# Squares to ScalarE, one power for 16 heads, routing in ten units, and the last batch's list and scatters moved into the experts

## The chip, the cores and the metric

The kernel runs on one core of one Trainium2 chip. The metric is the device time of one execution in microseconds (us); lower is better. A core has five engines with a queue of instructions each, worked off in order: TensorE (PE; its weight loads are listed as PEld), VectorE (DVE), ScalarE (ACT), GpSimd (POOL) and SyncE (SP), which issues transfers. They wait for each other by semaphores. GpSimd issues the indirect transfers (scatters) itself.

## What is computed

Four layers on X of 4 batches x 512 tokens x 256 columns: linear attention, a mixture of experts, softmax attention, and the same mixture again, each added to X. Cut to what matters here:

```python
# linear attention, 16 heads of 16 columns, chunks of 128 tokens
o = o * sigmoid(gate)
og = o.reshape(b, n, num_heads, hd)
og = og * rsqrt(mean(og * og, axis=-1, keepdims=True) + EPS)
x = x + (og.reshape(b, n, d) * w) @ Wo
# mixture of experts on layernorm(x): 32 experts, top 8 of a softmax, kept up to a mass of 0.8
logits = h @ gate_weight.T
combine = ...                      # weight of every token at every expert
for w_gu, w_d, ce in experts:
    g, u = split(h @ w_gu.T)
    acc = acc + (silu(g) * u) @ w_d.T * ce[:, None]
x = x + acc
```

## The kernel before

There are four stages, each with a block of its own and a barrier behind it: `lightning` (linear attention), `experts` "f", `attention`, `experts` "g".

`lightning` works through 4 batches (B) of 4 chunks (TT) of 128 tokens. A chunk has 4 units (QUADS), one for four heads, so there are 64 units, and 11 more in the drain (DRAIN), in which only `finish` and `route` run. Every engine has its own loop over the units; in a unit it does, in this order, its part of the scores, of `finish` and of the next half batch's projection, and then `route`. A chunk c is finished over the units of the following chunks: in unit 0 (q == 0) behind it ScalarE copies its outputs `o_t` (line 517); in unit 1 TensorE transposes them (434) and VectorE multiplies by the gate, `og` (709); in unit 2 GpSimd squares, `sq` (600); in unit 3 VectorE sums by head, `ss` and `ms` (723, 728). A chunk later GpSimd raises `ms` to -0.5, `rrms`, heads 0 to 7 in unit 0 and heads 8 to 15 in unit 1 (594); VectorE scales, `og` by `rrms` and `og_norm` by the weights, in unit 2 (715, 720); TensorE transposes `og_norm` in unit 3 (442) and ScalarE and VectorE split it into `og_t.hi` and `og_t.lo` (522, 697); TensorE multiplies by Wo, y (133), and VectorE adds it to X (702).

Score masks (`q_mask`) are made by GpSimd up to unit 39 and by ScalarE from unit 40 on (BY_ACT, lines 527 to 534 and 576 to 585).

The routing of a batch (`Routing`) is a list of steps 0 to 16. Step 0 and 2 are the layernorm (VectorE), step 1 its power `rstd` (GpSimd, 981), 4 and 5 transposes (TensorE, ScalarE), 6 the logits, 7 the softmax (ScalarE's exponential at 1032), 8 the choice, 9 and 10 the weights, 11 the counts (TensorE), 12 the rows' places `index` (VectorE, 1143 to 1152), 13 the tiles' counts, 14 to 16 the list of tiles that the experts read (`list_tiles`). In `lightning` batch f starts at unit 16 (f + 1) + 10, one step a unit (`steps_at`); 28 scatters (ALL) put its rows into `expert_rows` in DRAM (989), two a unit from 13 units after its start (PLACED). Batch 2's list and its first 8 scatters lie in the drain. The experts scatter the 20 left and route batch 3 beside their first pairs (`together`, `scatters_at` in `program`).

`experts` computes 144 tiles of 128 rows in 72 pairs. SyncE loads rows (1399), up to 8 pairs ahead. Three lists (PHASES) cover pairs 0 to 11, 12 to 25 and 26 to 71; the first needs the scatters of batches 0 and 1, the second those of batch 2, the third those of batch 3 and 32 stores of pad rows that SyncE issues four a pair from pair 17 on (1408). Results stay in a ring of 19 entries (RESULTS) until GpSimd scatters them, two scatters a pair (1304). GpSimd's queue in this stage is: power of batch 3, the scatters left of batch 2, the 28 of batch 3, then the results of pairs 0 to 60. VectorE (line 1540) waits before pair u until the results of pair u - 19 have landed:

```python
def wait_free(self, eng, u):
    if u >= RESULTS:
        eng.wait_ge(self.scattered[self.at(u)], 32 * (u // RESULTS))
```

## Time and profile before

| | us |
|---|---|
| median of 3 runs | 1091.12 |
| lowest and highest of them | 1089.68, 1091.18 |
| profiled execution, its own time | 1090.43 |
| span of that execution in the trace | 1088.70 |

Over the span TensorE is busy 877.9 us (81%), GpSimd 642.1 (59%), VectorE 583.0 (54%), ScalarE 544.2 (50%). These shares are means over stages with different limits. In the page's 40 slices of 27.2 us the first stage fills slices 0 to 10; in slices 9 and 10 TensorE is busy 2 and 5 tenths and its granted clock is 0.9 and 0.5 of full speed, while GpSimd is busy 7 to 8 tenths. In a timeline a row gives the start in us, the duration, the engine, the line in the kernel, the operation with output and input, and in brackets the engine's idle time before it and what ended that time. Rows of waits give the instruction that waited, what it waited for, the total in us, how often, and the longest.

### The profile page before, as it was taken

How to read it: one execution, taken by the hardware profiler on the slowest of the kernel's cores; microseconds unless marked ns; L12 is line 12 of the kernel's file. 1: busy time of each engine (PE TensorE's matmuls, PEld its weight loads, DVE VectorE, ACT ScalarE, POOL GpSimd, SP SyncE). 2: the span in 40 equal slices, each digit the busy share in tenths (PEclk: the TensorE clock that was granted, in tenths of full speed). 3: DMA queues.
4: the chain of work that ended last, by engine and by line, in shares of the span. 5: the costliest groups of instructions: out<-in, count | busy, mean ns of one | idle time of the engine just before them, and what ended most of it. 6: DMA issues, size and time to landing. Idle time of an engine off the chain costs nothing. (4 is left out here: it accounts for less than half of the span.)

```text
span 1088.7 us, 20645 instructions
## 1 busy us (share of the span) xinstructions
PE 877.9 (81%) x5504; PEld 665.9 (61%) x5504; DVE 583.0 (54%) x2104; ACT 544.2 (50%) x1084; POOL 642.1 (59%) x636
## 2 busy tenths in 40 slices
PE   5999998971489899999368998988758998999940
PEld 4666665641388699998233443544327887999830
DVE  4566785775373222226776488765535522222665
ACT  6333446640145455555268776766423554556520
POOL 2466648787577777775730010373754777777770
PEclk9999999995599999999679998988887999999975
DMA  9600002162578887773540110135326888778776
GB/s 335 252 1 2 1 20 91 67 240 78 168 233 301 281 267 220 222 259 123 174 136 35 34 35 35 49 121 215 116 103 200 261 303 280 227 218 255 270 243 204
DMA packets 93231, 181.64 MB, mean 167 GB/s; under 512 B 18985, under 2 KB 73788, under 8 KB 92736
## 3 DMA queue, kind: packets, MB, share of 16 engines
q1 hardware_dynamic: 68544, 114.19, 32.7%
q0 software_dynamic: 24576, 66.13, 16.7%
q8 instruction: 50, 0.82, 0.3%
q14 instruction: 61, 0.50, 0.2%
HBM read 96.34 MB, written 92.27 MB: 173 GB/s over the span
## 5 line engine op out<-in xcount | busy, mean ns | idle before, releaser
L1304 POOL DMA_INDIRECT result_rows<-ys,result_slots x288 | 286.6, 995 | 88.0 <-issue 81.0
L989 POOL DMA_INDIRECT expert_rows<-route_rows,index x224 | 223.0, 996 | 87.1 <-issue 68.0
L1955 ACT ACTIVATE b_probs<-ps 128x1024 f32<-128x1024 f32 x128 | 127.9, 1031 | 42.7 <-PE ps L1804 42.1
L1456 PE MATMUL ps<-w_gu,f_xts 128*128 x576 | 107.7, 331 | 3.3 <-ACT f_xts L1499 2.9
L1456 PE MATMUL ps<-w_gu,g_xts 128*128 x576 | 107.6, 330 | 2.9 <-ACT g_xts L1499 2.1
L1456 PEld LDWEIGHTS ps<-w_gu,f_xts 128*128 128x128 f32 x576 | 93.6, 193 | 4.5 <-issue 4.4
L1456 PEld LDWEIGHTS ps<-w_gu,g_xts 128*128 128x128 f32 x576 | 93.4, 193 | 4.3 <-issue 4.1
L1816 PE MATMUL ps<-b_probs,b_v_pad 128*32 128x512 f32 x512 | 78.4, 688 | 11.5 <-issue 5.4
L1549 DVE SCALAR_TENSOR_TENSOR g_h<-ps,g_xs,g_gate 128x96 f32<-128x96 f32 x144 | 39.1, 313 | 90.6 <-ACT g_gate L1506 87.7
L1549 DVE SCALAR_TENSOR_TENSOR f_h<-ps,f_xs,f_gate 128x96 f32<-128x96 f32 x144 | 39.2, 313 | 89.4 <-ACT f_gate L1506 88.3
L1517 ACT COPY ys<-ps 128x512 f32<-128x512 f32 x144 | 83.5, 580 | 1.9 <-PE ps L1475 1.9
L1321 DVE TENSOR_TENSOR parts<-parts 128x768 f32<-128x768 f32 (+2 forms) x96 | 66.3, 691 | 14.5 <-DMA parts<-result_rows 12.1
L1475 PE MATMUL ps<-f_w_d,f_hts 128*128 x288 | 74.1, 380 | 0.0
L1475 PE MATMUL ps<-g_w_d,g_hts 128*128 x288 | 74.1, 380 | 0.0
L1804 PE MATMUL ps<-b_q_t,b_k_t 64*128 64x512 f32 x256 | 63.2, 520 | 12.8 <-ACT b_probs L1955 10.4
L380 PE MATMUL ps<-a_q_mask,a_k_t 128*128 128x512 f32 x128 | 67.4, 609 | 5.5 <-POOL a_q_mask L585 3.6
L1499 ACT COPY f_xts<-ps 128x512 f32<-128x512 f32 x72 | 42.2, 586 | 58.0 <-PE ps L1444 57.1
L1499 ACT COPY g_xts<-ps 128x512 f32<-128x512 f32 x72 | 42.2, 586 | 49.8 <-PE ps L1444 48.5
L1804 PEld LDWEIGHTS ps<-b_q_t,b_k_t 64*128 64x128 f32 x256 | 24.7, 199 | 58.3 <-ACT b_probs L1955 27.8
L1444 PE MATMUL ps<-ident,f_xs 128*128 128x128 f32 x288 | 44.9, 280 | 16.4 <-DMA f_xs<-expert_rows 16.4
L594 POOL TENSOR_TENSOR a_rrms<-a_ms,a_root 128x8 f32<-128x8 f32 x32 | 54.1, 1690 | 6.8 <-DVE a_ms L728 6.3
L664 DVE TENSOR_TENSOR a_weights<-ps,a_decay 128x512 f32<-128x512 f32 x64 | 43.9, 686 | 24.6 <-PE ps L380 24.0
(362 smaller groups left out, 1824.6 us busy)
## 6 DMA issues: line engine op xcount, KB each, us to landing
parts<-result_rows SPq DMA_DIRECT2D x32, 896.0 KB, 4.8
f_xs<-expert_rows SPq DMA_DIRECT2D x144, 160.0 KB
g_xs<-expert_rows SPq DMA_DIRECT2D x144, 160.0 KB
expert_rows<-pad_rows SPq DMA_DIRECT2D x64, 160.0 KB
w_gu<-in_Wgu SPq DMA_DIRECT2D x1, 6144.0 KB, 18.7
expert_rows<-pad_rows SPq DMA_DIRECT2D x1, 5120.0 KB, 29.9
result_rows<-ys,result_slots POOLq DMA_INDIRECT x288, 3.1
f_w_d<-in_Wdown SPq DMA_DIRECT2D x1, 4096.0 KB, 15.3
```

What stands on the lines that cost most here:

```text
L380: nc.tensor.matmul(ps[:, bank_s + q % 2, :], k_t[:, q // 2, n * P:(n + 1) * P], q_mask[:, q % 2, :, :], start=True, stop=True).then_inc(sc ...
L989: self.nc.gpsimd.indirect_dma_start(xs, bass.IndirectOffsetOnAxis(self.index[:, f, t, r:r + 1].bitcast(U32), 0), self.x_rows(f)[:, t, :], ...
L1304: self.nc.gpsimd.indirect_dma_start(self.y_dram, bass.IndirectOffsetOnAxis(self.slots[:, i, j:j + 1].bitcast(U32), 0), self.ys[:, i, j, :] ...
L1321: self.nc.vector.tensor_tensor(parts[:, 0:pairs, :], parts[:, 0:pairs, :], parts[:, left:left + pairs, :], ALU.add).then_inc(self.folded, 1)
L1456: ins = nc.tensor.matmul(ps[:, bank_gu[u % 2], j * GU:(j + 1) * GU], xts[:, u % 2, o:o + P], w_gu[:, k, bass.ds(experts[j] * GU, GU)], sta ...
L1475: ins = nc.tensor.matmul(ps[:, bank_y[u % 2], j * D:(j + 1) * D], hts[:, u % 2, j * P:(j + 1) * P], w_d[:, bass.ds(experts[j] * D, D)], st ...
L1499: nc.scalar.copy(xts[:, u % 2, :], ps[:, bank_x[u % 2], :]).then_inc(xt_sb, 1)
L1517: nc.scalar.copy(results.ys[:, results.at(u), :, :], ps[:, bank_y[u % 2], :].rearrange("p (j n) -> p j n", j=2)).then_inc(y_ready, 1)
L1549: ins = nc.vector.scalar_tensor_tensor(out=h[:, u % 2, j, 0:INTER], in0=up, scalar=share, in1=gate[:, u % 2, j, :], op0=ALU.mult, op1=ALU. ...
L1804: ins = nc.tensor.matmul(ps[:, 2 * (u % 2) + j, :], k_t[rows, g, st * P:(st + 1) * P], q_t[rows, 2 * g + jp, :], start=True, stop=True)
L1816: ins = nc.tensor.matmul(ps[j * PAD:(j + 1) * PAD, bank_values, :], v_pad[:, st, g, :], probs[:, (2 * i + j // 2) % RING, j % 2, :], start ...
L1955: nc.scalar.activation(probs[:, u % RING, :, :], ps[:, 2 * (u % 2):2 * (u % 2) + 2, :], ACT.Exp, scale=float(HD) ** -0.5).then_inc(exp_don ...
```

## The change

In the first stage: the squares `sq` go from GpSimd to ScalarE (an activation, Square), still in unit 2 of the following chunk; the power `rrms` is one instruction for all 16 heads in unit 0; masks go to ScalarE from unit 36 on. The routing of batches 0 and 1 has its steps in 13 units in place of 15, and step 12 is at unit 9 in place of 12; the scatters of these batches start 10 units after the batch's start, one in the first unit of a chunk and two in the others, and come ahead of the routing's power in GpSimd's order. Batch 2 keeps steps 0 to 13 in the first stage (SPREAD_LAST).

In the experts: batch 2's list (steps 14 to 16) lies in units 4 to 6 of the first experts, all its 28 scatters are issued there (`scattered = 0`), and the steps 13 to 16 of batch 3 follow from unit 7. In `together` an empty unit is gone, which also holds for the second experts.

```diff
-    BY_ACT = 40
+    BY_ACT = 36
+    SPREAD = ((0, 1), (2,), (4,), (5,), (6,), (7,), (8,), (9, 11), (10,), (12,), (13, 14), (15,), (16,))
+    SPREAD_LAST = ((0, 1), (2,), (4,), (5,), (6,), (7,), (8,), (), (), (9, 11), (10,), (), (12,), (13,))
+    PLACED = 10
+    WITH_POWER = 3
...
         def steps_at(unit):
             for f in range(B - 1):
-                step = unit - (f + 1) * UNITS - FINAL
-                if 0 <= step < routing.STEPS:
-                    for part in routing.PARTS.get(step, (step,)):
-                        yield part, f
+                at, table = unit - (f + 1) * UNITS - FINAL, SPREAD_LAST if f == B - 2 else SPREAD
+                if 0 <= at < len(table):
+                    for step in table[at]:
+                        yield step, f
+
+        def sent_until(unit):
+            sent = 0
+            for f in range(B - 2):
+                begin = (f + 1) * UNITS + FINAL + PLACED
+                end = min(unit, begin + UNITS) if f < B - 3 else unit
+                for u in range(begin, end):
+                    if u < B * UNITS:
+                        sent += 1 if u % QUADS == 0 else 2
+                    elif u < B * UNITS + QUADS:
+                        sent += 1 if u < B * UNITS + WITH_POWER else 0
+                    else:
+                        sent += 2
+            return min(sent, (B - 2) * routing.ALL)
...
+                if q == 2 and exists(c - 1):
+                    act.wait_ge(og_ready, c)
+                    if some(c - 1):
+                        act.wait_ge(ss_ready, c - 1)
+                    nc.scalar.activation(sq[:, :], og[:, (n - 1) % 2, :], ACT.Square).then_inc(sq_ready, 1)
...
-                if q in (0, 1) and exists(c - 2):
-                    heads = slice(q * HH, (q + 1) * HH)
+                if q == 0 and exists(c - 2):
                     pool.wait_ge(ms_ready, c - 1)
                     if some(c - 2):
                         pool.wait_ge(scaled, c - 2)
-                    nc.gpsimd.tensor_tensor(rrms[:, heads], ms[:, heads], root[:, heads],
-                                            ALU.pow).then_inc(rrms_ready, 1)
-                if q == 2 and exists(c - 1):
...
+                    nc.gpsimd.tensor_tensor(rrms[:, :], ms[:, :], root[:, :], ALU.pow).then_inc(rrms_ready, 1)
...
             def route(unit):
+                for f, k in scatters_at(unit):
+                    routing.scatter(pool, f, k, xs_dram)
                 for step, f in steps_at(unit):
                     routing.gpsimd(pool, step, f)
-                for f, k in scatters_at(unit):
-                    routing.scatter(pool, f, k, xs_dram)
...
-        together = ((0, 1, 2, 4, 5, 6, 7), (8,), (9, 11), (10, 12), (), (13,), (14,), (15,), (16,))
+        together = ((0, 1, 2, 4, 5, 6, 7), (8,), (9, 11), (10, 12), (13,), (14,), (15,), (16,))
...
+        listed = ((14,), (15,), (16,))
+
+        def steps_at(u, held):
+            if held and placed <= u < placed + len(listed):
+                for step in listed[u - placed]:
+                    yield step, B - 2
+                return
+            at = u - len(listed) if held and u >= placed else u
+            if at < len(together):
+                for step in together[at]:
                     yield step, B - 1
...
-                    scattered = 8
+                    scattered = 0
```

## Rows read from the trace of the kernel before

**Rows 1.** Stages: length, busy PE, PEld, DVE, ACT, POOL, clock, DMA share, GB/s.
```profile
153.27:241.43 88.16, 74.45 (x519) 50.41 (x517) 63.78 (x224) 51.52 (x136) 70.26 (x63) 0.96 0.34 125
241.43:285.20 43.77, 9.41 (x52) 8.00 (x50) 21.50 (x110) 2.98 (x6) 30.32 (x29) 0.56 0.24 87
```

**Rows 2.** TensorE's waits from 153 to 242: for what, us in all, times, longest.
```profile
PE ps L442 <- DVE a_og_norm L720: 8.6, 5, 3.0
PE ps L380 <- ACT a_q_mask L534: 1.9, 3, 0.8
```

**Rows 3.** VectorE's waits in the same stretch.
```profile
DVE a_og L715 <- POOL a_rrms L594: 8.8, 3, 4.5
```

**Rows 4.** GpSimd by line from 153.27 to 241.43: busy, mean ns, idle before.
```profile
L594 POOL TENSOR_TENSOR a_rrms<-a_ms,a_root 128x8 f32<-128x8 f32 x12 | 20.3, 1689 | 0.3
...
L981 POOL TENSOR_TENSOR f_route_rstd<-f_route_var_eps,f_route_root 128x4 f32<-128x4 f32 x2 | 2.1, 1044 | 0.3 <-DVE f_route_var_eps L1050 0.3
```

**Rows 5.** GpSimd's timeline at the first stage's end: start, us, instruction, idle before it.
```profile
255.94 0.62 POOL L600 TENSOR_TENSOR a_sq<-a_og 128x256 f32<-128x256 f32 x1
...
265.83 1.67 POOL L594 TENSOR_TENSOR a_rrms<-a_ms,a_root 128x8 f32<-128x8 f32 x1
270.93 1.10 POOL L989 DMA_INDIRECT expert_rows<-route_rows,index  x1 [3.42 <-issue]
...
280.10 0.97 POOL L989 DMA_INDIRECT expert_rows<-route_rows,index  x1 [0.30 <-issue]
```

**Rows 6.** TensorE's timeline there.
```profile
241.01 0.43 PE L414 MATMUL ps<-a_weights,a_v_pad 128*32 128x128 f32 x8
...
273.15 0.55 PE L133 MATMUL ps<-a_w_o_hi,a_og_t_hi 128*128 128x256 f32 x1 [3.98 <-issue]
...
274.35 0.41 PE L133 MATMUL ps<-a_w_o_hi,a_og_t_lo 128*128 128x256 f32 x1
```

**Rows 7.** VectorE's timeline there, to the experts' first instruction.
```profile
254.09 0.53 DVE L1081 COPY f_route_key<-f_route_best 128x7 f32<-128x7 f32 x4
...
262.36 0.29 DVE L1138 TENSOR_TENSOR route_rows<-f_route_found,f_route_rmass 128x128 f32<-128x128 f32 x1
...
268.34 0.28 DVE L1143 TENSOR_TENSOR f_route_found<-ps,f_route_chosen 128x128 f32<-128x128 f32 x1
...
270.81 0.19 DVE L1207 TENSOR_TENSOR f_route_bound<-f_route_covered,f_route_whole 128x32 f32<-128x32 f32 x1
...
276.96 0.42 DVE L702 TENSOR_TENSOR X<-X,ps 128x256 f32<-128x256 f32 x1
285.20 0.17 DVE L1553 MEMSET f_h<- 128x128 f32 x1 [7.82 <-PEq L72]
```

**Rows 8.** GpSimd's timeline: first and last result scatter of the experts, then the attention.
```profile
350.55 0.97 POOL L1304 DMA_INDIRECT result_rows<-ys,result_slots  x1 [0.30 <-issue]
...
506.09 0.97 POOL L1304 DMA_INDIRECT result_rows<-ys,result_slots  x1 [0.31 <-issue]
516.78 0.10 POOL L807 MEMSET b_ln_root<- 128x4 f32 x1 [9.72 <-POOLq L72]
```

**Rows 9.** VectorE's timeline in the experts, pair 19.
```profile
357.19 0.28 DVE L1540 CAST result_slots<-f_xs 128x1 int32 x2 [1.54 <-DMA result_rows<-ys,result_slots]
```

**Rows 10.** SyncE's queue, its waits from 280 to 400.
```profile
SPq L1397 <- DMA expert_rows<-route_rows,index: 0.5, 1, 0.5
```

**Rows 11.** TensorE's waits from 355 to 390.
```profile
PE ps L1456 <- ACT f_xts L1499: 2.9, 3, 1.1
PE ps L1444 <- DMA f_xs<-expert_rows: 2.1, 4, 1.1
```

**Rows 12.** ScalarE by line from 30 to 245 us.
```profile
L507 ACT ACT_TABLE_LOAD x7 | 9.0, 1283 | 0.1
```

**Rows 13.** ScalarE by line in the attention, 516 to 812 us.
```profile
L1914 ACT ACTIVATE b_work<-ps 128x320 f32<-128x320 f32 x16 | 7.0, 438 | 13.8 <-PE ps L133 13.8
...
L1966 ACT ACT_TABLE_LOAD x1 | 1.3, 1283 | 0.0
```

22 lines of the change are left out of this document (6 added, 16 removed).

## The prediction

> **What bounds the kernel now.** I read the table of stages first, then who waited for whom, then the timelines of GpSimd, VectorE and TensorE around the seam between the first stage and the experts. A unit is one of the 64 score steps of the first stage, a chunk is four units, and t is time after the last output matmul of unit 63, which ends at 241.01 + 0.43 = 241.44 us [rows 6]. Up to there TensorE is busy 74.5 of 88.2 us; in the 43.8 us behind it, the drain, it is busy 9.4 and GpSimd 30.3 [rows 1].
>
> In units 40 to 63 TensorE waits 8.6 us for `og_norm` [rows 2], and in three of these waits VectorE itself stands at line 715 for the power `rrms`, 8.8 us in all [rows 3]: GpSimd does two powers of 1.69 us a chunk [rows 4] with scatters between them. In the drain the same queue is the pace. The square of chunk 15 starts at 255.94, its second power ends at 265.83 + 1.67 = 267.50, and the eight scatters of batch 2 run from 270.93 to 281.07 [rows 5]. VectorE's last sum ends at 277.38 and the next stage's first instruction is at 285.20 [rows 7]. So the last 3.7 us before the barrier are scatters alone, and before them VectorE waits for powers.
>
> In the experts GpSimd never pauses: the first result scatter is at 350.55, the last of the stage ends at 506.09 + 0.97 = 507.06, and the attention begins on it at 516.78 [rows 8]. VectorE already waits at 357.19 for the first results to land [rows 9]: pair 19 writes into the ring entry of pair 0 (19 entries).
>
> **The change part by part.** The sum is made against the profiled execution, 1090.43 us (its span of 1088.70 and 1.73 around it); the median of the runs shown is 0.7 higher.
>
> **Powers and squares.** A power of 8 columns costs 1.69 us and one of 4 columns 1.04 [rows 4]; 16 columns lie between one of them (1.7) and two (3.4), and the same slope of 0.16 a column gives 3.0, my estimate. That saves 0.4 us of GpSimd a chunk, and the square 0.6. What matters more is order: the power is ready one unit and two scatters earlier, since the second half no longer queues behind them. On ScalarE a square of 256 columns should cost under the 0.44 us of the 320 columns in the attention [rows 13]; it waits for VectorE's `og`, and behind it on ScalarE are the next projection's copy and the mask two units on, which TensorE needs later.
>
> **Scatters, units 36 to 63.** Seven in place of eight scatters a chunk at about 1.28 us each (350.55 to 506.09 in 121 steps [rows 8]), 9.0 us, with a power of 3.0 and about 0.8 for the smaller powers (one of 1.04 a batch [rows 4], one a half batch) make 12.8 us of GpSimd a chunk, against 8 x 1.28 + 2 x 1.69 + 0.6 + 0.8 = 15.0 before. A chunk of TensorE's own work here is about 74.5 / 6 = 12.4 us [rows 1], so GpSimd stops being late by more than a few us. Moving `rstd` behind the unit's two scatters can hold VectorE's step 2 by 2.6 us, twice in this stretch. The masks of units 36 to 39 go to ScalarE, whose masks cost TensorE at most 0.8 us a wait [rows 2], so 0 to 3 us; I take 0.5. Of the 8.6 us I count back the three waits that VectorE's row blames on GpSimd, about 6, and the lower clock behind them (granted 0.96 on the mean, so lowered in part of the stretch [rows 1]), about 1.5; against this stand 1 for `rstd` and 0.5 for the masks. VectorE is busy 63.8 of 88 us here [rows 1] and takes over about 2 us more routing before unit 64, so the gain can be nothing, and at most 10. **-6 us (0 to -10).**
>
> **The drain.** After the change GpSimd has here two powers and about seven scatters, no square and nothing of batch 2. VectorE works in order: it waits for ScalarE's exponential of step 7 (a table load of 1.28 us [rows 12] and 0.3) until t = 1.4, ends step 7 at 2.8, `og_t.lo` 3.2, step 8 at 7.0 (3.8 us), `og` of chunk 15 at 7.3; ScalarE's square is done at 7.8. Two products of chunk 14 and a sum of X to 8.5, `ss` and `ms` of chunk 15 at 9.1. The power of chunk 15 follows at once, to 12.1, because the three scatters of units 64 to 66 and the power of chunk 14 need only 3.8 + 3.0 us before it. VectorE meanwhile has steps 9 and 10; steps 8 to 10 took 254.09 to 262.65 less 0.9 of other work, 7.7 us [rows 7], so it is at 13.5. Products of chunk 15 to 14.3, X to 14.7, steps 12 and 13 (268.34 to 270.81, 2.5 us [rows 7]) to 17.2, `og_t.lo` 17.6, the six matmuls of y (273.15 to 274.76, 1.6 us [rows 6]) with their hand-over to 19.8, X to 20.3. The list of batch 2 (270.81 to 276.96, 6.1 us [rows 7]) is gone from here. GpSimd's last four scatters end at 12.1 + 5.1 = 17.3. Before, the last scatter ended 4.1 us ahead of 285.20 [rows 5, 7]; the next stage then starts at 17.3 + 4.1 or 20.3 + 2 to 4, say t = 23.3, in place of 285.20 - 241.44 = 43.8. **-20.5 us (-14 if VectorE's routing spreads out, -24 if the barrier is short).**
>
> **The experts.** Eight scatters come in ahead of the results: 8 x 1.28 = 10.2 us on an engine that doesn't pause there. Counted from the stage's start, the wait for the first result's landing [rows 9] ends 10.2 us later, so the hidden product of pair 19 and TensorE behind it stand up to 10.2 us. Behind it TensorE waited 2.1 and 2.9 us for rows that SyncE loaded late beside the 32 pad stores [rows 11]; SyncE runs on during the stall, so these 5.0 are covered: 10.2 - 5.0 = 5.2. The end goes by GpSimd: 507.06 + 10.2 = 517.3, and 4.1 to the barrier's end, 521.4 against 516.78, 4.6. The load of pair 12, which waited 0.5 us for the last scatter of batch 2 [rows 10], moves by 10 us; with eight buffers ahead of TensorE this is just hidden, but it puts the pad stores some 5 us later. The moved list is VectorE work in pairs 4 to 6, before the stall, and is swallowed by it. **+5 us (0 to +12; 12 where nothing is covered and TensorE comes back at the low clock).** In the second experts the table only closes an empty unit: 0 (-1 to +1).
>
> Sum: -6 - 20.5 + 5 = -21.5, 1090.43 - 21.5 = 1068.9, and 0.7 for the median: **1069.6 us.**
>
> **A rule against this change.** All 16 squares of the attention (line 1914) run between 128 exponentials with one table load in the whole stage [rows 13], so a square needs no load beside the exponential's table; the first stage works with other tables, the gate's sigmoid for one, loaded seven times in its middle [rows 12], and there no row shows a square. The Trainium skill, ScalarE: Activation LUTs, section "Table sets: the hidden batching unit", says that tables come in sets, that cheap functions (it names relu, copy, identity, abs) are in every set, and that one from another set costs a load; the square is not among those it names. By that rule the square could bring loads here; by the rows of the attention it does not.
>
> **The rivals.**
> - **VectorE keeps the first stage (0.10).** For it: it is 72% busy before the drain [rows 1] and the routing is packed closer. Then units 40 to 63 gain nothing and the drain 14: 1091.1 - 14 + 5 = 1082.
> - **The stall in the experts isn't covered (0.10).** For it: the pads start later too. Against: SyncE needs nothing of the stalled engines while it has buffers. +12 in place of +5: 1077.
> - **Squares switch ScalarE's table (0.05), the slower case.** Place: ScalarE in unit 2 of each chunk. Price: a load before and one after each of 16 squares, 16 x 2 x 1.28 [rows 12] = 41 us. It decides once more than 21.5 of the 41 lie on the path, which ScalarE's masks would bring about from unit 36 on; all of it gives 1111. Against it: rows 13.
> - **Nothing to measure (0.03).** The same loads, with about half of them on the path: 1069.6 + 21 = 1091.
>
> **How the numbers follow.** My forecast holds 0.72, so 1069.6. Range: 1059, near the far ends of all three terms (-10 - 24 + 0 would be 1057), to 1082, the first rival; the second lies inside. Left out are the slower case, the tie and some of the tails. A measurement of this kernel can tell about 0.2%, 2 us, from no change. Faster by more: 0.92; within: 0.03; slower: 0.05.
>
> **What would show it.** In the changed kernel: VectorE's waits at the product with `rrms` all but gone; a power of 16 columns near 3.0 us; no table load at the squares' line; the first stage's last scatter before VectorE's last sum, and the experts' first instruction near 256 to 260 us in place of 285; one wait of about 10 us for a landed result at pair 19 and hardly any for loaded rows after it; the attention some 21 us earlier and nothing changed from there. Wrong would be: table loads around squares, VectorE waiting for `rstd`, or a first stage of the old length before the drain.

## The result and the profile after

The changed kernel takes 1080.91 us (median of 11 runs, 1075.53 to 1086.24) where the kernel before takes 1089.68 on the same chip (1086.65 to 1092.55): ratio 0.9914, 95% interval 0.9893 to 0.9935. It is faster, by 8.8 us; the forecast was 21.5. A second measurement, run as the experiment e13 below, gives 0.9900 (0.9867 to 0.9932).

Its profiled execution took 1081.71 us, 1079.9 of them span. The page's line of busy time, first of the kernel before, then of the changed one (share of the span, instructions):

```profile
PE 877.9 (81%) x5504; PEld 665.9 (61%) x5504; DVE 583.0 (54%) x2104; ACT 544.2 (50%) x1084; POOL 642.1 (59%) x636
```
```profile
span 1079.9 us, 20627 instructions
PE 883.9 (82%) x5504; PEld 670.5 (62%) x5504; DVE 581.2 (54%) x2104; ACT 554.6 (51%) x1116; POOL 627.0 (58%) x600
```

GpSimd has 15 us less, ScalarE 10 more, as the moved squares and masks and the merged powers make it. TensorE has 6 us more with the same 5504 matmuls, so some of them ran slower. In the profile of e13, the same kernel again, it has 876.3 us, so these 6 us are that execution's; what both show comes next.

I split the span at the three points that the prediction used: the end of the output matmul of unit 63 (t = 0), the experts' first instruction, and the attention's first.

| | before | changed | changed again (e13) | forecast |
|---|---|---|---|---|
| start to t = 0 | 241.44 | 246.98 (+5.5) | 244.87 (+3.4) | -6 |
| drain | 43.76 | 22.00 (-21.8) | 22.09 (-21.7) | -20.5 |
| first experts | 231.58 | 241.43 (+9.9) | 238.51 (+6.9) | +5 |
| attention and second experts | 571.9 | 569.5 (-2.4) | 569.7 (-2.2) | 0 |
| span | 1088.7 | 1079.9 (-8.8) | 1075.2 (-13.5) | -21.5 |

The drain is what was forecast. The stretch ahead of it is not.

**Ahead of t = 0.** ScalarE copies each chunk's output once (16 copies, which time the stage well). The changed kernel against the kernel before, start of the copy in us:

| copy | 6 | 7 | 8 | 9 | 10 | 12 | 14 | 15 | 16 |
|---|---|---|---|---|---|---|---|---|---|
| before | 97.68 | 111.21 | 124.27 | 140.99 | 155.48 | 186.71 | 217.88 | 230.53 | 241.51 |
| changed | 98.66 | 114.17 | 130.02 | 149.14 | 163.09 | 193.14 | 221.79 | 232.23 | 248.34 |
| later by | 1.0 | 3.0 | 5.8 | 8.2 | 7.6 | 6.4 | 3.9 | 1.7 | 6.8 |

So 7.2 us are lost between copies 6 and 9 (units 24 to 36; the recorded expectations count these copies' units from 1, so 25 to 37), 6.5 are won from there to copy 15 (unit 60), and 5.1 are lost from there to copy 16. That copy runs 1.4 us behind t = 0 here and 0.1 before, so up to t = 0 the last chunk loses 3.8. In e13 the three are 5.6 lost, 5.8 won and 2.7 lost. The middle part is as large as the gain I had priced. These are TensorE's waits of the changed kernel in the first losing stretch, 98.66 to 149.2 us (for what, us in all, times, longest), and the windows of the two last chunks of this stretch (length, busy PE, PEld, DVE, ACT, POOL, granted clock, DMA share, GB/s):

```profile
PE ps L396 <- POOL a_q_mask L606: 3.6, 3, 1.7
PE ps L1030 <- DVE f_route_total L1111: 1.8, 1, 1.8
PE ps L405 <- DVE a_k_dec L667: 1.5, 1, 1.5
```
```profile
114.17:130.02 15.85, 15.38 (x108) 11.13 (x108) 8.06 (x22) 8.69 (x15) 7.49 (x7) 1.00 0.01 2
130.02:149.14 19.12, 15.74 (x96) 9.95 (x95) 17.67 (x80) 6.66 (x16) 6.69 (x4) 0.82 0.01 1
```

The second of these chunks in e13:

```profile
130.01:147.51 17.50, 14.12 (x96) 8.80 (x95) 16.48 (x78) 6.53 (x17) 5.45 (x4) 0.90 0.00 1
```

Batch 0's routing stands here in units 26 to 35, packed. TensorE waits 1.8 us at the routing's counting matmul (line 1030) for a total that VectorE had only just been asked for, and 1.5 for `k_dec` because VectorE itself stands at the exponential of the step before. The granted clock is 0.82 on the mean of this chunk (0.90 in e13, with the same waits): behind the two waits, from 138 to 144 us, it is 0.50 to 0.52, the lower of its two levels, 1.2 GHz. The waits that the prediction counted, for `og_norm` [rows 2], are down from 8.6 us in five waits to 0.6 in two (1.2 in e13). Another wait has grown: behind copy 9 TensorE waits 5.3 us for ScalarE's masks, in e13 too, where it waited 1.9 before [rows 2] (window 149.2 to 247 us):

```profile
PE ps L396 <- ACT a_q_mask L555: 5.3, 3, 2.4
```

The last chunk, TensorE's timeline (start, us, instruction, idle before it): it stands for the rows of batch 2, and its next matmuls run slowly.

```profile
231.73 0.43 PE L430 MATMUL ps<-a_weights,a_v_pad 128*32 128x128 f32 x8 [1.01 <-DVE a_weights L677]
234.58 1.12 PE L1017 MATMUL ps<-ident,route_rows 128*128 128x128 f32 x4 [2.42 <-DVE route_rows L1071]
```

Line 1017 is step 4 and stands one unit behind step 2, which writes these rows; before the change it stood two units behind.

**The drain.** The windows (columns as above; the second answers the second of [rows 1]), GpSimd's two powers and its last scatter, and VectorE's last sum and the experts' first instruction, of the changed kernel:

```profile
149.20:246.98 97.78, 86.56 (x606) 59.52 (x604) 69.61 (x238) 61.94 (x164) 71.46 (x60) 0.97 0.34 125
246.98:268.98 22.00, 8.38 (x35) 6.94 (x34) 14.09 (x80) 3.08 (x6) 13.06 (x9) 0.59 0.16 60
```
```profile
247.00 2.94 POOL L614 TENSOR_TENSOR a_rrms<-a_ms,a_root 128x16 f32<-128x16 f32 x1
...
255.00 2.94 POOL L614 TENSOR_TENSOR a_rrms<-a_ms,a_root 128x16 f32<-128x16 f32 x1 [1.25 <-DVE a_ms L741]
...
262.25 0.98 POOL L1002 DMA_INDIRECT expert_rows<-route_rows,index  x1 [0.30 <-issue]
```
```profile
265.03 0.42 DVE L715 TENSOR_TENSOR X<-X,ps 128x256 f32<-128x256 f32 x1 [1.76 <-PE ps L133]
268.98 0.17 DVE L1566 MEMSET f_h<- 128x128 f32 x1 [3.53 <-PEq L72]
```

GpSimd works 13.1 us here in place of 30.3 and is done 2.2 us ahead of VectorE; the list and 15 of 22 scatters are gone [rows 5, 7].

**The powers and the squares.** GpSimd and ScalarE in the first stage, by line (busy, mean ns, idle before; for ScalarE min, median and max):

```profile
L614 POOL TENSOR_TENSOR a_rrms<-a_ms,a_root 128x16 f32<-128x16 f32 x16 | 47.8, 2986 | 19.7 <-DVE a_ms L741 19.5
```
```profile
L538 ACT ACTIVATE a_sq<-a_og x16: 404/417/439, 41.5 to 253.3; 128x256 f32<-128x256 f32 x16
```

**The experts.** GpSimd's first and last result scatter and the attention's first instruction (they answer [rows 8]); SyncE's waits (they answer [rows 10]); VectorE's waits for landed results:

```profile
344.86 0.97 POOL L1317 DMA_INDIRECT result_rows<-ys,result_slots  x1 [0.31 <-issue]
...
500.94 1.50 POOL L1317 DMA_INDIRECT result_rows<-ys,result_slots  x1 [0.30 <-issue]
510.41 0.10 POOL L820 MEMSET b_ln_root<- 128x4 f32 x1 [7.96 <-POOLq L72]
```
```profile
SPq L1410 <- DMA expert_rows<-route_rows,index: 10.6, 1, 10.6
SPq L1417 <- DVE tab L1280: 1.0, 1, 1.0
```
```profile
DVE result_slots L1553 <- DMA result_rows<-ys,result_slots: 10.0, 4, 4.9
```

The first result scatter comes 75.9 us after the stage's start, 10.5 later than before (65.4), and stays so. What TensorE makes of it I read from ScalarE's gates (the activation behind a pair's first product), one a pair. How much later a gate runs than before, each counted from its own stage's start:

| pair | 3 | 7 | 9 | 12 | 20 | 21 | 23 | 24 | 26 to 71 |
|---|---|---|---|---|---|---|---|---|---|
| changed | 0.2 | 1.5 | 3.7 | 5.2 | 5.2 | 6.2 | 6.2 | 9.5 | 9.8 |
| changed again (e13) | 0.2 | 1.3 | 3.0 | 5.3 | 5.6 | 6.9 | 5.8 | 6.6 | 5.8 |

From pair 26 on both run at TensorE's own 2.82 us a pair. So the loss is made by pair 26, in two places: 5 us in pairs 6 to 12, where VectorE now makes two lists, and the rest in pairs 20 to 26: 4.6 us in the first profile and 0.5 in e13.

### The profile page after: what moved, and what is told of

It is laid out like the page before. It is cut to its first block and busy times, and to the rows that moved or that the text cites. A ratio compares the mean times of both kernels' runs of the same rounds, so it can differ in the third digit from the quotient of the medians.

```text
span 1079.9 us, 20627 instructions
## 1 busy us (share of the span) xinstructions
PE 883.9 (82%) x5504; PEld 670.5 (62%) x5504; DVE 581.2 (54%) x2104; ACT 554.6 (51%) x1116; POOL 627.0 (58%) x600
## 5 line engine op out<-in xcount | busy, mean ns | idle before, releaser
L1317 POOL DMA_INDIRECT result_rows<-ys,result_slots x288 | 290.8, 1010 | 87.9 <-issue 80.6
L1829 PE MATMUL ps<-b_probs,b_v_pad 128*32 128x512 f32 x512 | 75.2, 661 | 11.0 <-DVE b_v_pad L2101 5.5
L614 POOL TENSOR_TENSOR a_rrms<-a_ms,a_root 128x16 f32<-128x16 f32 x16 | 47.8, 2986 | 19.7 <-DVE a_ms L741 19.5
L606 POOL TENSOR_TENSOR a_q_mask<-a_q_t,a_head_rows 128x512 f32<-128x512 f32 x36 | 37.4, 1048 | 34.0 <-PE ps L396 30.1
```

The source lines that it names most:

```text
L1317: self.nc.gpsimd.indirect_dma_start(self.y_dram, bass.IndirectOffsetOnAxis(self.slots[:, i, j:j + 1].bitcast(U32), 0), self.ys[:, i, j, :] ...
L1829: ins = nc.tensor.matmul(ps[j * PAD:(j + 1) * PAD, bank_values, :], v_pad[:, st, g, :], probs[:, (2 * i + j // 2) % RING, j % 2, :], start ...
```

## The experiments

**Theories.** The forecast missed almost only in the stretch before t = 0, so the first question is what makes units 24 to 36 and the last chunk late: the packed routing (theory), or GpSimd's longer power and ScalarE's squares (rival). The second is what the experts' loss consists of: the list, GpSimd's ring of results, or SyncE's pads. The third came up on the way: what the first part of the change is worth alone. All stage times below are from one profiled execution each; the medians are over all runs. The kernel before had medians of 1089.6 us beside e1 to e4, 1089.7 beside e5 to e8, 1090.8 beside e9 to e11 and 1092.2 beside e12, e13 and e14.

| | t = 0 | drain | first experts | rest | median | ratio to before |
|---|---|---|---|---|---|---|
| before | 241.44 | 43.76 | 231.58 | 571.9 | | |
| changed | 246.98 | 22.00 | 241.43 | 569.5 | 1080.9 | 0.9914 (0.9893 to 0.9935) |
| e1 | 244.37 | 22.07 | 238.60 | 572.4 | 1080.1 | 0.9904 (0.9873 to 0.9936) |
| e2 | 237.19 | 39.41 | 232.11 | 569.7 | 1081.1 | 0.9921 (0.9887 to 0.9954) |
| e3 | 244.63 | 23.30 | 239.77 | 573.9 | 1082.5 | 0.9925 (0.9887 to 0.9963) |
| e4 | 244.01 | 30.69 | 236.61 | 573.7 | 1086.0 | 0.9956 (0.9929 to 0.9983) |
| e5 | 241.20 | 24.52 | 239.38 | 568.5 | 1077.9 | 0.9885 (0.9841 to 0.9928) |
| e6 | 240.44 | 25.04 | 238.59 | 572.3 | 1078.2 | 0.9882 (0.9839 to 0.9924) |
| e7 | 244.74 | 23.30 | 241.28 | 570.8 | 1081.9 | 0.9917 (0.9887 to 0.9947) |
| e8 | 244.93 | 23.26 | 240.57 | 570.5 | 1081.8 | 0.9930 (0.9906 to 0.9954) |
| e9 | 238.18 | 27.71 | 238.50 | 571.5 | 1079.7 | 0.9901 (0.9869 to 0.9933) |
| e10 | 237.05 | 41.94 | 230.96 | 572.3 | 1083.3 | 0.9935 (0.9911 to 0.9959) |
| e11 | 243.57 | 26.22 | 238.11 | 571.7 | 1083.6 | 0.9938 (0.9915 to 0.9960) |
| e13 | 244.87 | 22.09 | 238.51 | 569.7 | 1079.9 | 0.9900 (0.9867 to 0.9932) |
| e14 | 239.40 | 25.29 | 239.91 | 571.4 | 1079.3 | 0.9883 (0.9847 to 0.9920) |

Where no code differs the columns still differ: the rest lies between 568.5 and 573.9, t = 0 of one and the same code up to there (changed, e3, e4, e7, e8, e13) between 244.0 and 247.0, the first experts of the changed kernel at 241.4 and 238.5. The drain of one code agrees best, within 0.1 us (changed, e13) to 0.8 (e5, e14). So differences under some 3 us in the columns of t = 0 and the first experts, under 1 in the drain and under 5.5 in the rest are no finding by themselves.

### e1: batch 0's routing spread out again

```
+    SPREAD_FIRST = ((0,), (1,), (2,), (), (4,), (5,), (6,), (7,), (8,), (9,), (10,), (11,), (12,), (13, 14), (15, 16))
-                at, table = unit - (f + 1) * UNITS - FINAL, SPREAD_LAST if f == B - 2 else SPREAD
+                at, table = unit - (f + 1) * UNITS - FINAL, (SPREAD_FIRST, SPREAD, SPREAD_LAST)[f]
-                begin = (f + 1) * UNITS + FINAL + PLACED
+                begin = (f + 1) * UNITS + FINAL + (13 if f == 0 else PLACED)
```

> The changed kernel, but batch 0's routing goes back to one step a unit (units 26 to 40), so its scatters begin at unit 39 and five of the 56 fall to the drain. In the changed kernel ScalarE's eighth-but-one copy of o (the ninth of 16, unit 37) starts at 149.14 us against 140.99 before, 8.2 later, and the copy of unit 25 only 1.0 later. Theory, packing: the loss arises because steps that need each other stand in neighbouring units (0 and 1 in one, then 2, then 4; 7 behind 6; 11 behind 8), so that TensorE waits (3.6 us for masks behind rstd and the power, 1.5 for k_dec while VectorE stands for the exponential, 1.85 for the total of step 8) and works on at a granted clock of 0.82. Then that copy starts at 141 to 143 here, the output matmul of unit 63 ends 5 to 8 us earlier than the changed kernel's 246.98, the drain is 2 to 5 us longer (five scatters of 1.28 us more), and the time is 1 to 5 us below the changed kernel's, ratio to before 0.987 to 0.991. Rival, GpSimd's 3.0 us power in front of its masks, or ScalarE's squares: the copy stays at 147 to 150, and the time is 2 to 5 us above the changed kernel's.

The ninth copy starts at 140.87 us, where the kernel before has it (140.99). The two chunks of the windows above, in e1 (columns as there):

```profile
112.17:125.21 13.04, 13.04 (x92) 9.15 (x92) 9.84 (x27) 7.07 (x14) 7.93 (x7) 1.00 0.01 2
125.21:140.87 15.66, 13.09 (x101) 8.87 (x102) 10.50 (x44) 8.24 (x17) 4.92 (x4) 1.00 0.01 1
```

The clock stays at 1.00, and the same chunk takes 15.66 us in place of 19.12. So the packing made the lateness of the ninth copy: the theory holds there, in every run (with batch 0 packed the ninth copy is at 146.1 to 149.1, in seven profiles; spread, at 140.3 to 142.6, in nine). But t = 0 is only 2.6 us earlier than the changed kernel's first profile has it, not 5 to 8, and 0.5 earlier than e13's. Of the 8.3 us of copy 9 (6.6 against e13) 5.1 are left at copy 15 (4.1): a late chunk catches up in the units behind it, so the losses and gains above can't simply be added. The rest goes in the last chunk, which takes 17.2 us to t = 0 in place of 14.8 (13.6 in e13). TensorE stands 5.15 us at the turning of batch 2's rows, and VectorE in front of it 2.82 for `rstd`:

```profile
230.76 1.43 DVE L1072 TENSOR_SCALAR route_rows<-X,f_route_mean_var,f_route_rstd 128x256 f32<-128x256 f32 x4 [2.82 <-POOL f_route_rstd L995]
```

One thing in my expectation was wrong as code: the scatters of batches 0 and 1 overlap in units 52 to 54 and catch up there, up to four a unit, so no more of them fall to the drain than in the changed kernel, and it is as long (22.07).

### e2: squares and one power alone

The kernel before with the first part of the change (ScalarE's square, one power of 16 columns), nothing else.

```
+                    nc.scalar.activation(sq[:, :], og[:, (n - 1) % 2, :], ACT.Square).then_inc(sq_ready, 1)
...
-                    nc.gpsimd.tensor_tensor(rrms[:, heads], ms[:, heads], root[:, heads],
-                                            ALU.pow).then_inc(rrms_ready, 1)
...
+                    nc.gpsimd.tensor_tensor(rrms[:, :], ms[:, :], root[:, :], ALU.pow).then_inc(rrms_ready, 1)
```

> The kernel before with one part of the change: the square on ScalarE and one power of 16 columns; routing, masks, scatters and experts as before. Theory (my term for units 40 to 63, without the rest of the change): the 8.6 us of TensorE's waits for og_norm in units 40 to 63 fall under 2, ScalarE's ninth copy of o stays within 1.5 us of 140.99, the output matmul of unit 63 ends at 233 to 238 in place of 241.44, and the drain (43.8) is 1 to 4 us shorter because the last power follows the square sooner. Time 5 to 11 us below before, ratio 0.990 to 0.995. Rival: the power of 3.0 us in front of GpSimd's masks, or the squares in front of ScalarE's copies, are what made units 25 to 37 of the changed kernel 8 us late; then the ninth copy is 4 to 8 us late here too, and the ratio is 0.997 to 1.003.

The ninth copy is at 141.19: the long power and the squares aren't what makes units 24 to 36 late; the rival falls. t = 0 comes 4.25 us sooner, and TensorE's waits from 153 us to it show why (compare [rows 2]):

```profile
PE ps L380 <- ACT a_q_mask L539: 1.9, 3, 0.8
PE ps L442 <- DVE a_og_norm L717: 1.8, 2, 1.2
```

The drain is 4.35 shorter. The ratio, 0.9921, is nearly that of the whole change (0.9914 and 0.9900, with intervals that overlap): everything else in it, with 17 us off the drain, adds so little that these runs can't tell it from nothing.

### e3: the list back in the drain

```
-    SPREAD_LAST = ((0, 1), (2,), (4,), (5,), (6,), (7,), (8,), (), (), (9, 11), (10,), (), (12,), (13,))
+    SPREAD_LAST = ((0, 1), (2,), (4,), (5,), (6,), (7,), (8,), (), (), (9, 11), (10,), (), (12,), (13, 14), (15, 16))
...
-                        lambda u: steps_at(u, not final),
+                        lambda u: steps_at(u, False),
```

> The changed kernel, but batch 2's list (steps 14 to 16) goes back into the drain; all 28 scatters of batch 2 stay in the experts. The drain gets 4 to 7 us longer (the list's VectorE time was 6.1 us before, rows 7). In the changed kernel the gate of pair 13 of the experts runs 5.2 us later than before, counted from the stage's start, and every pair from 26 on 9.8 later. Theory: pairs 7 to 13 are late because VectorE runs two lists in the pair loop, but from pair 22 on later clocks count, which this edit leaves: GpSimd's result scatters (10.5 later) and SyncE's pad stores, which begin behind the load of pair 12 that waits for batch 2's last scatter. Then pair 13 is 0 to 1.5 us late here and pairs from 26 on still 6 to 9.5, and the time is 2 to 6 above the changed kernel's. Rival, the list itself is the cause: pairs from 26 on are only 3 to 5 late, and the time is that of the changed kernel within 2 us.

The list makes the drain 1.3 us longer, not 4 to 7: VectorE has time for it while the last y is made. In the experts pair 13 is 1.5 late, as the theory had it, then pair 20 is 4.7, pair 21 6.7, and all from 26 on 7.1. VectorE now stands longer for landed results:

```profile
DVE result_slots L1553 <- DMA result_rows<-ys,result_slots: 13.0, 4, 8.4
```

So without the list in the way TensorE runs into the ring of results that much harder: the list's 5 us are swallowed, as the prediction said, and what is left at pair 26 is 7.1 beside 5.8 to 9.8 with the list. The time, 1.5 us above the changed kernel's, doesn't tell the theory from the rival.

### e4: eight scatters back in the drain

```
-            return min(sent, (B - 2) * routing.ALL)
+            sent = min(sent, (B - 2) * routing.ALL)
+            return sent + 2 * min(4, max(0, unit - (B * UNITS + 7)))
...
-                    scattered = 0
+                    scattered = 8
```

> The changed kernel, but eight of batch 2's 28 scatters go back to the end of the drain, where they stood before; the list stays in the experts. Eight scatters of 1.28 us behind step 12 make the drain 6 to 9 us longer. In the experts GpSimd is then where it was before, and the load of pair 12 no longer waits. Theory: the list in pairs 7 to 13 still costs 5.2 us at pair 13, and part of it is then swallowed by what TensorE waits for anyway at pairs 20 to 26: pairs from 26 on 3 to 6 us later than before in place of 9.8; time 1 to 5 above the changed kernel's. Rival, GpSimd's ten us are the whole of the 9.8 and the list is swallowed: pairs from 26 on 0 to 1 late, and the time within 2 of the changed kernel's or below it.

The drain is 8.6 us longer than e13's. GpSimd's first result scatter is back at 65.0 us, and pairs 12 to 20 are 4.6 late, from 26 on 5.1. So moving eight scatters out of the drain saves 8.6 there and costs some 2 in the experts (238.51 against 236.61, no more than one code differs): the move pays. The rival, that GpSimd is all of the loss, falls. But the theory's "swallowed" didn't happen either: TensorE arrives 4.6 us later at pair 20 and waits for loaded rows all the same. SyncE shows why: its first pad store stands 52.5 us after the stage's start (47.5 before), since it waits 5.3 us for batch 2's list at pair 12 and then for the next.

### e5, e6, e9: the last batch's routing

e5 is e1 with GpSimd's routing step ahead of the unit's scatters again:

```
-                for f, k in scatters_at(unit):
-                    routing.scatter(pool, f, k, xs_dram)
                 for step, f in steps_at(unit):
                     routing.gpsimd(pool, step, f)
+                for f, k in scatters_at(unit):
+                    routing.scatter(pool, f, k, xs_dram)
```

> The kernel of e1 (batch 0's routing one step a unit), and GpSimd takes its routing step, the power rstd, ahead of the unit's scatters again, as before the change. In e1 the output matmul of unit 63 ends at 244.37 us, though its copy of o in unit 61 starts where that of e2 does (227.16 against 227.05) and e2 ends at 237.19: TensorE waits 5.2 us for the routing rows of batch 2, VectorE ahead of it 2.8 us for rstd, and TensorE then works at the low clock (0.81 on the mean of 226 to 244). Theory: rstd behind the scatters is the 2.8 of it; here VectorE doesn't wait, TensorE's wait falls to 2 to 2.8 (as in e3 and e4, 2.4), and unit 63 ends 2 to 4 us sooner than in e1, 240.5 to 242.5. Time 1076 to 1079. Rival, the steps 0, 1, 2, 4 in neighbouring units are all of it: the wait stays over 4 and the end within 1.5 us of e1's.

VectorE waits 0.4 us for `rstd` and TensorE 2.7 for the rows; t = 0 is 3.2 us sooner than in e1 (5.0 in e14, the same kernel), as expected. The order was half of it. e6 adds an empty unit between steps 2 and 4:

```
-    SPREAD_LAST = ((0, 1), (2,), (4,), (5,), (6,), (7,), (8,), (), (), (9, 11), (10,), (), (12,), (13,))
+    SPREAD_LAST = ((0, 1), (2,), (), (4,), (5,), (6,), (7,), (8,), (), (9, 11), (10,), (), (12,), (13,))
```

> The kernel of e5, and batch 2's routing gets one empty unit between step 2 (the rows, VectorE) and step 4 (TensorE turns them), so steps 4 to 8 come one unit later; step 9 and what follows stay. Theory: TensorE's wait for the rows (2.4 us in e3, e4 and the changed kernel) goes, and with it the low clock behind it, so the output matmul of unit 63 ends 3 to 6 us sooner than in e5, at 236 to 239.5, where e2 has it (237.19); the drain is 0 to 3 us longer, since steps 7 and 8 (VectorE, 3.8 us in the sum) move into it. Time 1072 to 1077. Rival, the routing's work itself in units 58 to 63 is what costs, wherever it stands: the end within 2 us of e5's.

t = 0 moves by 0.8 us, not 3 to 6. The wait for the rows is gone, and one of 2.4 for `q_dec`, which VectorE makes behind the rows, is in its place. The theory falls; with VectorE behind both waits it is the suspect that is left. e9 puts steps 0 to 8 back to one a unit:

```
-    SPREAD_LAST = ((0, 1), (2,), (), (4,), (5,), (6,), (7,), (8,), (), (9, 11), (10,), (), (12,), (13,))
+    SPREAD_LAST = ((0,), (1,), (2,), (), (4,), (5,), (6,), (7,), (8,), (9, 11), (10,), (), (12,), (13,))
```

> The kernel of e6, but batch 2's steps 0 to 8 stand in units 58 to 66 one a unit, as before the change (0 and 1 no longer in one unit); step 9 and what follows stay in units 67 to 71. In e6 the output matmul of unit 63 ends at 240.44 us and the experts begin at 265.48; in e2, with these steps as here, it ends at 237.19. Theory: step 1's power rstd gets a unit to run before VectorE's step 2 wants it, so the wait of 2.4 us that TensorE has in e6 behind VectorE goes; unit 63 ends at 236.5 to 238.5, the drain is 25 to 27.5, the experts begin at 262.5 to 265. Time 1073 to 1077. Rival: steps 6 to 8, now all behind unit 63, lengthen the drain by as much as is won: the experts begin at 265 to 267, the time is that of e6 within 1.5.

t = 0 is at 238.18, where the theory had it, 2.3 sooner than e6's, and the drain is 2.7 longer, so the experts begin at 265.89: the rival. Seen together, t = 0 goes from 238.2 to 241.2 in e5, e6, e9 and e14 while the experts begin at 264.7 to 265.9. What ends the drain there doesn't depend on t = 0; that it is the last batch's routing on VectorE, from the sum of unit 58 on, fits but was not tried apart.

### e7 and e8: the ring, and the pads

e7 is e3 with `RESULTS = 20` for 19.

> The kernel of e3 (batch 2's list in the drain, all its scatters in the experts) with 20 entries in the ring of results in place of 19. In e3 pairs 12 to 19 of the experts are 1.5 us later than before, counted from the stage's start, pair 20 is 4.7 later, pair 21 6.7, and all from 26 on 7.1. Theory, the ring sets it: GpSimd's first result scatter comes 10.3 us later than before, pair 19 needs the entry of pair 0; one entry more gives a pair of lead, 2.82 us, so pairs 21 to 26 and all after them are 4 to 5 late in place of 7.1, and the time is 1.5 to 3 below e3's. Rival, SyncE's pads (they begin at 52.2 in place of 47.5 and go at 5.3 us a round whatever TensorE does) set it: pairs 20 and 21 are less late, but from 26 on it is 6 to 7.5 as in e3.

Pairs from 26 on are 9.7 late, later than in e3 (but no further apart than one code was: 5.8 and 9.8 in the two profiles of the changed kernel). The ring's wait is mostly gone (3.3 us in one wait), and TensorE waits for loaded rows instead, 6.2 us in five waits between 328 and 370 us. The theory falls: one entry more wins nothing, and with the ring longer the named waits are those for loads. e8 splits the pads between SyncE and ScalarE (the lines added stand in ScalarE's loop and issue on its queue):

```
-    PADS = 4
+    PADS = 2
...
+                if PADS_AT <= u < PADS_AT + E // (2 * PADS):
+                    store_pads(E // 2 + PADS * (u - PADS_AT), PADS)
```

> The kernel of e7, and the 32 pad stores are issued half by SyncE (two a pair) and half by ScalarE, each in eight rounds from pair 17, so that SyncE's rounds get shorter (four pads take it 2.1 of 5.3 us, a load 0.9). Theory: in e7 whatever lateness is left from pair 24 on beyond the ring's comes from loads that stand behind the pads; here TensorE's waits for loaded rows at pairs 20 to 26 (3.4 us in e3, 2.1 before) fall under 1.5, and pairs from 26 on are 2 to 4 late, or less, since the kernel before has the same waits. Time 1 to 3 below e7's. Rival: two DMA issues a pair on ScalarE, about 1 us beside its 1.7 us of work a pair, hold its copies up and cost as much as is gained; pairs 17 to 25 get late evenly, and from 26 on it is as in e7 or more.

Pairs 21 to 24 come down to 2.7 to 4.0 late, but pair 25 is 7.7 and all from 26 on 8.9: neither the theory's 2 to 4 nor the rival's even delay. SyncE's queue is the surprise. It issues two pads in place of four, and but for one round of 4.0 us its rounds are still 4.8 to 5.9 us long (start, us, instruction); of these rounds, 319 to 359 us, the trace names 4.9 us as waits, for a free buffer. The DMA engines meanwhile are busy 98% of the time (window, columns as above). Behind its last pads SyncE stands 4.8 us at the load of pair 26, until all 32 stores have landed (last line; 0.7 before):

```profile
334.90 0.90 SPq L1421 DMA_DIRECT2D expert_rows<-pad_rows  x2
337.75 0.89 SPq L1412 DMA_DIRECT2D f_xs<-expert_rows  x2
339.72 1.85 SPq L1421 DMA_DIRECT2D expert_rows<-pad_rows  x2
343.29 1.02 SPq L1412 DMA_DIRECT2D f_xs<-expert_rows  x2
345.66 1.00 SPq L1421 DMA_DIRECT2D expert_rows<-pad_rows  x2
```
```profile
338.19:358.19 20.00, 15.67 (x89) 12.45 (x87) 4.38 (x22) 8.56 (x21) 15.12 (x17) 1.00 0.98 334
```
```profile
SPq L1408 <- DMA expert_rows<-pad_rows: 4.8, 1, 4.8
```

That suggested a third theory: the bytes.

### e12: more bytes in the same pairs

The kernel before, and 16 stores more, on ScalarE's queue:

```
...
+                if PADS_AT <= u < PADS_AT + E // PADS:
+                    for j in range(2 * (u - PADS_AT), 2 * (u - PADS_AT) + 2):
+                        nc.scalar.dma_start(spare[j * P:(j + 1) * P, :],
                                            routing.tables.pad_rows[:, :]).then_inc(spare_stored, 16)
...
```

> The kernel before, and ScalarE issues 16 more stores of 160 KB (the pad rows into a memory of their own that nothing reads), two a pair beside SyncE's pads in pairs 17 to 24, in both experts. In e8 SyncE issued half as many pads, yet its rounds still took 5.0 us, and the DMA engines were 97 to 99% busy there. Theory, what the DMA engines move sets pairs 20 to 26: 16 x 0.164 MB at about 320 GB/s are 8 us more, so pairs from 26 on come 5 to 10 us later than before, counted from the stage's start. Rival, SyncE's own issue sets them: pairs from 26 on within 1.5 us of before.

Pair 18 is 0.2 us late, pair 20 5.1, pair 24 9.4, all from 26 on 9.5; in the second experts 6.1 from pair 24 on. The whole took 1100.62 us in its one run, beside 1092.17 of the kernel before (median of 11). The same window of both kernels (332 to 372 us), first before, then e12:

```profile
332.00:372.00 40.00, 36.36 (x227) 32.80 (x224) 10.68 (x52) 21.19 (x52) 30.52 (x32) 1.00 0.92 309
```
```profile
332.00:372.00 40.00, 34.18 (x203) 30.79 (x201) 9.31 (x46) 18.96 (x45) 30.56 (x32) 0.94 0.96 331
```

SyncE issues what it issued, but its eight rounds of pads begin over 41.7 us in place of 36.7. ScalarE's issues don't hold up its copies: TensorE waits 3.1 us for them, as before (2.9 [rows 11]), and 5.5 for loaded rows (2.1). So these named waits grow by 3.6 of the 9.5 us; the rest falls where the granted clock is 0.80 to 0.84 (353.85 to 393.85 us), which was 1.00 before. So SyncE's number of issues doesn't set pairs 20 to 26 (e8); what the DMA engines have to move does, with 32 pad stores of 160 KB, the pairs' rows, and the results (e12). In the changed kernel this crowd begins 5.8 us later (first pad 53.3 us after the stage's start, 47.5 before), because SyncE stands 10.6 us for batch 2's scatters at the load of pair 12 (in e4, without that, 6.4 us for the two lists).

The traces show what that shift is worth. In the runs with the list moved and a granted clock of 1.00 in every 5 us from 60 to 110 us of the stage (e4, e5, e6, e13, e14) the first pad is 4.5 to 5.7 us late and pair 26 4.4 to 6.0. In the changed kernel's first profile, e3, e7 and e8 the first pad is 4.7 to 6.3 late but pair 26 7.1 to 9.8, and in each the clock falls to 0.50 to 0.70 in at least one of these stretches; e1, e9 and e11 lie between (0.67 to 0.75, pair 26 4.2 to 6.9). The changed kernel's two profiles, 4.0 us apart at pair 26, agree on the first pad (53.3 and 53.2 us) and nearly on the last round (91.1 and 90.1), and differ in TensorE's waits for rows (4.9 and 2.5 us) and in the clock (0.66 in one stretch, and 1.00 throughout). What sets such a profile apart from its twin is not shown.

### e10 and e11: the power alone, and the change without its first part

e10 is the kernel before with one power of 16 columns; the square stays on GpSimd.

> The kernel before with one power of 16 columns in place of two of 8; the square stays on GpSimd. With both (e2) unit 63 ends 4.25 us sooner and the drain is 4.35 shorter. Theory, the order of GpSimd's queue: the power is whole one unit and two scatters earlier, so most of e2's gain is here: unit 63 ends at 237.5 to 239.5, the drain is 40 to 42.5, the ratio 0.993 to 0.997. Rival, the square on ScalarE is what gains: unit 63 ends within 1 us of 241.44, the drain is over 43, the ratio 0.998 to 1.002.

t = 0 is 4.4 us sooner, as much as with the squares (e2), though the stage's first copy runs 2.2 us later here. The drain is 1.8 shorter (4.35 in e2), the ratio 0.9935. So the power's order is enough for the gain before t = 0; the square's place shows in the drain, 2.5 us between these two profiles. e11 is the changed kernel with squares and two powers on GpSimd.

> The changed kernel with the squares and two powers of 8 columns on GpSimd, as before: the change without its first part. Theory: GpSimd is late again in units 36 to 63, since seven scatters, a square and two powers a chunk are 9.0 + 0.6 + 3.4 + 0.8 = 13.8 us against 12.4 of TensorE's own work, so what the changed kernel wins back between the ninth copy (8.2 late) and the fifteenth (1.7 late) isn't won back: unit 63 ends at 249 to 254, the drain is 23 to 27; time 1086 to 1094. Rival, seven scatters in place of eight are enough, and square and powers don't matter any more: unit 63 ends at 244 to 247.5, as in the changed kernel and in e3, e4, and the time is 1079 to 1083.

t = 0 is at 243.57, no later than with them (244.87 in e13); the rival. With seven scatters a chunk GpSimd isn't late any more, whoever squares: TensorE's waits for `og_norm` behind the ninth copy are 1.9 us in two, where it waited 8.6 before [rows 2]. The drain is 4.1 us longer than e13's. So the first part is worth 8.5 us alone (1089.6 - 1081.1) and some 4 in the drain beside the rest (the ratios, 0.9938 against 0.9914 and 0.9900, overlap): both parts cure the same lateness of GpSimd.

### e13 and e14: the changed kernel again, beside a repaired one

e14 is the kernel of e5 once more.

> The changed kernel itself, a second time. In its first profile the ninth copy of o is at 149.14 us, unit 63 ends at 246.98 and the first experts take 241.4; in four runs with the same first stage (e3, e4, e7, e8) the ninth copy is at 146.1 to 146.8 and unit 63 ends at 244.0 to 244.9; in e1, e6, e9 with the same experts these take 238.5 to 238.6. Theory: some 2.5 us in either place are that one execution's, and here unit 63 ends at 244 to 245 and the experts take 238 to 239.5, the span 1076 to 1079. Rival: they are the kernel's, and the first profile's numbers come again within 1 us.

> The kernel of e5 beside the changed kernel on the same chip: the changed kernel, with batch 0's routing one step a unit and rstd ahead of the scatters. Theory: unit 63 ends at 241 to 242, 3 us sooner than in e13, so the time is 1.5 to 4 us below that of e13 and the ratio to before 0.986 to 0.991. Rival: what is won before unit 63 is given back in the drain (in e5 it took 24.5 us in place of 22), and the two are within 1 us.

e13: t = 0 at 244.87 and first experts 238.51, as the theory had them; the span of 1075.2 is just under its 1076 to 1079. Of the first profile's loss before t = 0 some 2 us, and of its loss in the experts some 3, are that execution's; the waits behind the loss are the same (1.9 us for the total, 1.5 for `k_dec`, 3.6 for masks). e14: t = 0 at 239.40, 5.5 us sooner than e13, but the experts begin only 2.3 sooner and take 1.4 longer. The medians are 1079.3 and 1079.9, within 1 us: the rival. Three measurements of e5, e6 and e14 give 0.988, two of the changed kernel 0.990 and 0.991; the intervals overlap, so it is not shown that the repair beats the change.

## Why the prediction was wrong, point by point

- **First stage, -6 (measured +5.5 and +3.4): the step that failed.** Its mechanism was right: the 8.6 us of waits for `og_norm` went, because the power is whole earlier, and alone that is 4.3 us (e2, e10). But the sum began at unit 36. The change also packs batch 0's routing into units 26 to 35, where the sum had no term: by copy 9 it cost 7.2 us (5.6 in e13), 6.9 us of waits where the kernel before has 3.5 (97.68 to 141 us), and the low clock behind them (e1). And the only price I put on the packing was 1 us for `rstd`, for which VectorE didn't wait in the changed kernel; the last chunk lost 3.8 us up to t = 0 (2.7 in e13), with a wait of 2.4 us for the packed steps 0, 1, 2, 4, in these two profiles a low clock behind it (0.77 and 0.87 from copy 15 to t = 0, 1.00 before), and step 6's 16 matmuls, 2.0 us, that stand before t = 0 now. The term of 0.5 us for masks was too small as well: TensorE waits 5.3 us for ScalarE's masks in place of 1.9, 4.7 with the squares back on GpSimd (e11), and 1.9 in e2 and e10, so the squares aren't the cause; which of the routing, scatters and masks is was not tried. The bounds (0 to -10) held no loss, though the diff showed work moving up on an engine that TensorE waits for. How much of the +3.4 to +5.5 each place makes stays open, since a chunk's lateness is partly caught up behind it: with batch 0 spread out t = 0 moves by 0.5 to 2.6 us (e1), with `rstd` ahead of the scatters too by 3.7 to 7.6 (e5 and e14 against both profiles). I had looked at VectorE's busy share, which doesn't show how soon a step's result is asked for.
- **Drain, -20.5 (measured -21.8, -21.7): right,** and by its own steps. The end was put at t = 23.3 and is at 22.0; GpSimd's last scatter ends at 17.3 (16.2), VectorE's last sum at 20.3 (18.5), a power of 16 columns at 3.0 (2.99). That nothing of the list belongs there was worth less than I thought, 1.3 us (e3).
- **Experts, +5 (0 to +12; measured +9.9, +6.9): the size within its range, the steps half right.** GpSimd came 10.5 us later, the load of pair 12 stood 10.6, the list was swallowed (e3). What failed is "SyncE runs on during the stall, so these 5.0 are covered": SyncE was itself held, its pads began 5.8 us later, and the DMA engines then had the same bytes to move (e12), so TensorE waited for rows as before, 4.9 us in the first profile and 2.5 in e13 (2.1 [rows 11]). There was no single wait of 10 us for a landed result, but four of 10 in all, because the list had already made TensorE 5 us late when pair 19 came: the list ate up part of the stall where the sum had the loads do it. That e13 comes out near +5 is in part luck.
- **Second experts, 0:** -2.3 in attention and second experts together, within what unchanged code varies there.
- **Squares and ScalarE's table: right.** The stage loads tables 23 times before and after, none at the squares' line; a square takes 0.42 us. By the rule of the Trainium skill (ScalarE: Activation LUTs, section "Table sets: the hidden batching unit") a square could have cost a load; no trace here shows one.
- **The rival with 1082** came closest by its time and was another story: the first stage did keep its length, but VectorE is no busier than before (69.6 of the 97.8 us before t = 0, 63.8 of 88.2 [rows 1]), and the drain gained 22, not 14. The measured 1080.9 lies in the range only because that rival had set its end.

The sum: -21.5 forecast; with the first stage's term at the +3.4 to +5.5 that the two profiles show, it would have been -12.1 to -10.0, against -8.8 (first median) and -12.3 (second).

## What to carry to other kernels

When a change packs steps that depend on each other closer together, price every place where it does so, also where nothing was late before: look at the distance between a step's result and its first reader, not only at how busy the engine is, and then at what waits next (in e6 one unit more of distance moved the wait to another reader). Measure the parts of a change alone: here its first part (a merged power, squares elsewhere) gave 8.5 us by itself where the whole gave 8.8 and 12.3, since both halves cured the same lateness and the second brought losses of its own. Profile the same kernel twice: some 2 us of the first profile's loss before t = 0 and 3 of its loss in the experts were that execution's. And a transfer that is moved behind a wait takes its bytes along: where the DMA engines are as busy as here (92 to 98%), what is late is the whole crowd behind it.

## What the runs showed of the hardware

- A wait of TensorE can cost more than its length: with 3.3 us of waits in a chunk the granted clock was 0.82 over 19.1 us and the chunk had 15.7 us of busy TensorE, in e13 with the same waits 0.90 and 14.1, and in e1 without them 1.00 and 13.1. It doesn't always: in e11 a wait of 2.3 us for the rows in the last chunk left the clock at 1.00 (231.65 to 243.57 us), where the changed kernel, with 2.4, has 0.77 and e13 0.87.
- SyncE's rounds of a pair's load and its pads took 4.8 to 5.9 us, one 4.0, with two stores of 160 KB (and as many on ScalarE's queue; e8) and 4.9 to 6.2 with four (changed kernel); 16 stores more on another engine's queue made TensorE 9.5 us late, and 6.1 in the second experts, at 331 GB/s in place of 309 (e12).
- GpSimd's power of 16 columns takes 2.99 us, as the slope of those of 4 and 8 had it [rows 4].
